# Sorting rounds 1 to 3 of a mixture of experts in two sets of four blocks, beside a recurrent mixer, on one Trainium2 core

## What is computed

```python
xn = layernorm(x)
# mixer
prev = shift_by_one_token(xn); xx = prev - xn
lin = lambda mix, W: (xn + xx * mix) @ W.T          # six of them: r, w, k, v, a, g
r, alpha, g = sigmoid(...), sigmoid(...), sigmoid(...); decay = exp(-softplus(...)); k = tanh(...)
state = state * decay + alpha * k * v               # along the 256 tokens of a sequence
mixed = r * state
mn = group_norm(mixed, 16 groups of 8 channels) * gn_w + gn_b
s = (mn * g) @ W_out.T + b_out
# experts
cur = xn
for r in range(4):
    logits = cur @ Wg[r] + bg[r]
    cw = softmax over the best two logits, 0 for the other two experts
    y_e = gelu(cur @ W1[e] + b1[e]) @ W2[e] + b2[e]  # for each expert e
    cur = cur + sum_e cw[:, e] * y_e
out = x + s * silu(cur)
```

## Time and profile before

| | us |
|---|---|
| runs, median of 3 | 808.48 (805.29 to 808.94) |
| profiled execution | 802.44 |
| its span | 800.7 |
| PE busy in the span | 757.6 |
| DVE, ACT busy | 623.9, 613.9 |
| POOL busy | 198.8 |

### The profile page before, as it was taken

One profiled execution on the slowest core, in us unless ns is written; L12 is line 12 of the kernel. 1 busy time (PEld: TensorE's weight loads), 2 busy tenths in 40 slices (PEclk: granted clock), 3 DMA queues, 4 the chain that ended last, 5 costly groups with the idle time before them and its releaser, 6 DMA issues.

```text
span 800.7 us, 9933 instructions
## 1 busy us (share of the span) xinstructions
PE 757.6 (95%) x3250; PEld 591.2 (74%) x3250; DVE 623.9 (78%) x1035; ACT 613.9 (77%) x858; POOL 198.8 (25%) x223
## 2 busy tenths in 40 slices
PE   8999999999999999999999999999889799758796
PEld 7778777877877777787788778777666677646675
DVE  7999876897896897788788689857699378568456
ACT  7989787887887887788788778778577687466574
POOL 1122111111111111111111111111563016555844
PEclk9999999999999999999999999999979999969898
DMA  8567965332644326533264322644113869949742
GB/s 261 145 120 185 229 154 113 56 97 40 158 107 94 52 40 145 120 92 53 56 143 106 93 39 52 160 100 100 42 41 114 234 197 282 309 130 266 197 128 59
DMA packets 80220, 102.25 MB, mean 128 GB/s; under 512 B 40366, under 2 KB 52138, under 8 KB 76970
## 3 DMA queue, kind: packets, MB, share of 16 engines
q1 hardware_dynamic: 60314, 63.80, 26.3%
q0 software_dynamic: 19440, 37.56, 24.9%
q10 hardware_dynamic: 416, 0.26, 0.1%
HBM read 44.85 MB, written 8.73 MB: 67 GB/s over the span
## 4 chain that ended last, share of the span: by engine, by line
PE 71%; DVE 9%; issue 6%; DMA 4%; ACT 4%; POOL 4%; SPq 1%; POOLq 0%; DVEq 0%; ACTq 0%
PE h_bank L1627 11%; PE h_bank L1631 11%; PE h_bank L1628 11%; PE y_bank L1728 10%; PE y_bank L1716 10%; PE y_bank L1718 10%; PE p_bank L1834 5%; DMA cur<-tmp 4%; DVE g_lo L1294 2%; ACT g L865 2%; ACT g_hi L871 2%; POOL out L744 1%; DVE tmp L1313 1%; POOL cw_b L735 1%; PE r_bank L1766 1%
## 5 line engine op out<-in xcount | busy, mean ns | idle before, releaser
L1294 DVE TENSOR_TENSOR g_lo<-g,g_hi 128x1024 fp32r<-128x1024 f32 x242 | 292.6, 1222 | 142.4 <-ACT g_hi L871 139.6
L865 ACT ACTIVATE g<-h_bank,b_all 128x512 f32<-128x512 f32 x416 | 265.8, 681 | 55.4 <-PE h_bank L1631 54.7
L871 ACT ACTIVATE g_hi<-g 128x1024 fp32r<-128x1024 f32 x242 | 256.8, 1061 | 7.6
L775 POOL DMA_DIRECT2D cur<-tmp x96 | 83.4, 869 | 494.1 <-DVE tmp L1313 330.7
L1627 PE MATMUL h_bank<-cur_hi,w_all 128*128 128x512 f32 x416 | 184.2, 443 | 0.2 <-ACT cur_hi L917 0.2
L1631 PE MATMUL h_bank<-cur_lo,w_all 128*128 128x512 f32 x416 | 163.7, 393 | 0.0
L1628 PE MATMUL h_bank<-cur_hi,w_all 128*128 128x512 f32 x416 | 163.4, 393 | 0.0
L1716 PE MATMUL y_bank<-g_hi,w_all 128*128 128x512 f32 x408 | 157.5, 391 | 0.0
L1718 PE MATMUL y_bank<-g_hi,w_all 128*128 128x512 f32 x392 | 152.6, 389 | 0.0
L1728 PE MATMUL y_bank<-g_lo,w_all 128*128 128x512 f32 x408 | 111.1, 393 | 4.4 <-DVE g_lo L1294 4.4
L1627 PEld LDWEIGHTS h_bank<-cur_hi,w_all 128*128 128x128 f32 x416 | 78.7, 189 | 32.7 <-issue 17.3
(11 more groups left out here) (238 smaller groups left out, 733.8 us busy)
## 6 DMA issues: line engine op xcount, KB each, us to landing
cur<-tmp POOLq DMA_DIRECT2D x113, 256.0 KB
cw_b<-cw_scratch SPq DMA_DIRECT2D x25, 1024.0 KB, 5.8
staged<-w_all SPq DMA_DIRECT2D x34, 512.0 KB
cw_b<-sorted_gates SPq DMA_DIRECT2D x17, 256.0 KB
xn_t<-cur SPq DMA_DIRECT2D x8, 256.0 KB, 5.9
cur<-in_x SPq DMA_DIRECT2D x7, 256.0 KB, 5.3
bench<-sorted_rows SPq DMA_DIRECT2D x6, 266.0 KB, 6.1
xn_scratch<-bench POOLq DMA_DIRECT2D x6, 256.0 KB, 3.1
```

The costliest lines, as they stand in the source:

```text
L775: pool.dma_start(cur[:, block_of(turn_of(s))], tmp[:, s % SUMS, :], accum_op=ALU.add).then_inc(summed, DMA)
L865: nc.scalar.activation(g[:, gb, ft * BLK:(ft + 1) * BLK], hb[ft][:, :], ACT.Gelu_apprx_tanh, bias=bias_of(s1, ft)).then_inc(gelu_done, 1)
L871: nc.scalar.activation(g_hi[:, gb, h], g[:, gb, h], ACT.Copy).then_inc(g_hi_done, 1)
L1294: nc.vector.tensor_tensor(g_lo[:, gb, h], g[:, gb, h], as_f32(g_hi[:, gb, h]), ALU.subtract).then_inc(g_lo_done, 1)
```

## The change

Rounds 1 to 3 are all sorted, in two **sets** of four blocks (blocks 0 to 3 and 4 to 7), so there are six sorts (`SORTS`), n = 0 to 5; sort n is for set n % 2 in round n // 2 + 1. Each list has 2 x 4 + 5 = 13 items (`LIST`) where four blocks have 16 steps. Round 0 stays dense: steps 0 to 31. The six lists follow, steps 32 to 109. While the list of one set runs, the other set is sorted: `after(n)` is the last step whose sum set n needs, and every part of sort n stands at a fixed distance behind it, the first item at `after(n) + 14`. With it come these changes:

- Mixers start every 10 steps; all eight `s` go to memory as rows, and all of the output is written by scatters.
- ACT writes `cur_hi` of a block that comes back, straight from the bank (`take_back`); DVE writes only `cur_lo`. ACT takes the squares of the group norm (`squares`) and its scale and shift (`scale_normed`), with waits of DVE on ACT and of ACT on DVE in between.
- DVE adds no sums any more: POOL does all, and scatters the four tiles of one block in each of four steps.
- Ranks stand at `after + 3` between the two halves of low parts, pairs and scores behind `combine` of that step, gates and places behind `combine` of the next, the list at `after + 6`. The places are scanned over 96 counts and not 144, `match` has 208 elements and not 408.
- PE loads 13 slot numbers ahead of `down` two steps before each list (`load_slots`); SP loads 13 expert and 13 gate numbers, POOL 13 block numbers, for each list.
- Gathers of `s` and `x` for set 0 stand behind steps 87, 88, 91 and 92, those for set 1 behind 100 to 103.

The diff, cut:

```diff
-SORTED = 6
-ITEMS = 2 * SORTED + 5
-TURNS = R * NB - SORTED
-FIRST_ITEM = E * (TURNS - 1)
-LAST_AT = FIRST_ITEM + ITEMS
-STEPS = LAST_AT + E
+SET = 4
+SORTS = 2 * (R - 1)
+LIST = 2 * SET + 5
+ITEMS = SORTS * LIST
+FIRST_ITEM = E * NB
+STEPS = FIRST_ITEM + ITEMS
...
-MIX_AT = (15, 26, 37, 48, 59, 70, 84, 102)
+MIX_AT = tuple(15 + 10 * m for m in range(NB))
...
-BATCHES = [(0, 2), (2, 2)] + [(k, QUADS) for k in range(QUADS, TURNS - 2, QUADS)] + [(TURNS - 2, 1), (TURNS - 1, 1)]
+BATCHES = [(0, 2), (2, 2), (4, QUADS)]
...
+def sums_for(n, j):
+    return E * (SET * n + j + 1) if n < 2 else first_step(n - 2) + items_through(j)
+
+def after(n):
+    return sums_for(n, SET - 1) - 1
...
+SORT_AT = {n: after(n) + 2 for n in range(SORTS)}
+PAIR_AT = {n: after(n) + 3 for n in range(SORTS)}
+PLACE_AT = {n: after(n) + 4 for n in range(SORTS)}
+LIST_AT = {n: after(n) + 6 for n in range(SORTS)}
+ROW_AT = {(n, j): after(n) + 4 + j for n in range(SORTS) for j in range(SET)}
+BACK_END = {(n, j): after(n) + (11, 12, 13)[j // 2 + j % 2] for n in range(SORTS) for j in (0, 1, 3)}
+BACK_MID = {(n, 2): after(n) + 13 for n in range(SORTS)}
+GATES_AT = {(n, h): after(n) + 12 + 2 * h for n in range(SORTS) for h in range(2)}
+SPLIT_SORTED_AT = {(n, j): after(n) + (12, 13, 15, 16)[j] for n in range(SORTS) for j in range(SET)}
+SILU_AT = {(n, j): first_step(n) + items_through(j) + 1 for n in (SORTS - 2, SORTS - 1) for j in range(SET)}
+SILU_AT.update({(SORTS - 2, j): first_step(SORTS - 1) + j - 1 for j in (1, 2, 3)})
+SILU_AT[SORTS - 1, SET - 1] = None
...
+GATHER_AFTER = {(SORTS - 2, 0): 87, (SORTS - 2, 1): 88, (SORTS - 2, 2): 91, (SORTS - 2, 3): 92,
+                (SORTS - 1, 0): 100, (SORTS - 1, 1): 101, (SORTS - 1, 2): 102, (SORTS - 1, 3): 103}
...
             for s in range(STEPS - ADDED_BY_DVE):
...
-                if s in ADDED_BY_DVE_AT:
-                    continue
...
                 pool.wait_ge(combined, s + 3)
                 if s > 0:
+                    pool.wait_ge(summed, DMA * s)
+                for n in range(SORTS):
+                    if s == first_step(n):
+                        pool.wait_ge(listed, n + 1)
+                        regs = [pool.alloc_register(f"block{n}_{i}") for i in range(LIST)]
+                        pool.load(regs, tables[0:1, n % 2, T_BLOCK, 0:LIST])
...
+                for n, j in at_step(ROW_AT, s):
+                    scatter_rows(n, j)
+                for n, j in at_step(SILU_AT, s):
+                    pool.wait_ge(row_out, OUT_ORDER.index((n, j)) + 1)
+                    scatter_out(n, j)
+                for n, j in at_step(GATHER_AFTER, s):
+                    gather_sx(n, j)
...
-            def take_back(j):
+            def take_back(n, j):
...
+                nc.scalar.activation(cur[:, block_of(SET * (n % 2) + j)], rb[:, :], ACT.Copy)
...
+                nc.scalar.activation(cur_hi[:, q, :], rb[:, :], ACT.Copy).then_inc(r_empty, 1)
...
+            def squares(m):
+
+                act.wait_ge(centred, m + 1)
+                nc.scalar.activation(sq[:, :, :], cen[:, :, :], ACT.Square).then_inc(squared, 1)
+
+            def scale_normed(m):
+
+                act.wait_ge(mn_ready, m + 1)
+                act.wait_ge(dve_consts, 1)
+                nc.scalar.activation(gn[:, :, :], mn_t[:, :, :], ACT.Identity, bias=gnb2[:, :], scale=gnw4[:, :]).then_inc(normed, 1)
...
             def mixer_squares(m):
 
-                link(nc.vector.tensor_tensor(sq[:, :, :], cen[:, :, :], cen[:, :, :], ALU.mult))
+                dve.wait_ge(centred, m + 1)
+                dve.wait_ge(squared, m + 1)
...
+            def load_slots(n):
+
+                regs = [pe.alloc_register(f"slot{n}_{i}") for i in range(LIST)]
+                pe.wait_ge(listed, n + 1)
+                pe.load(regs, tables[0:1, n % 2, T_SLOT, 0:LIST])
...
+                pe.wait_ge(r_empty, bank_job("sort_logits", n))
+                pe.wait_ge(summed, DMA * sums_for(n, SET - 1))
+                tokens = cur[:, n % 2 * SET * BLK:(n % 2 + 1) * SET * BLK].rearrange("p (m i r) -> p i m r", i=D // RP, r=RP)
                 for i in range(D // RP):
+                    last = nc.tensor.matmul(rb[RP * i:RP * (i + 1), :], wg_p[:, n // 2 + 1, :], tokens[:, i, :, :], start=True, stop=True)
```

More of the change, by code:

```diff
@@ L94 @@
 COUNTS = len(PAIRS) * COLS
 ROW = D + E + 1
[L96 to L110, removed]
@@ new lines @@
+SILU_AT[SORTS - 1, SET - 1] = None
+IDS_AT = {n: after(n) + 15 for n in (SORTS - 2, SORTS - 1)}
+GATHER_AFTER = {(SORTS - 2, 0): 87, (SORTS - 2, 1): 88, (SORTS - 2, 2): 91, (SORTS - 2, 3): 92,
+                (SORTS - 1, 0): 100, (SORTS - 1, 1): 101, (SORTS - 1, 2): 102, (SORTS - 1, 3): 103}
+OUT_ORDER = sorted((key for key, s in SILU_AT.items() if s is not None), key=SILU_AT.get)
+MID, END = 0, 1
+BANK_TIMES = {("logits", n, 0): (s, MID if n == 0 else END) for n, s in LOGITS_AT.items()}
+BANK_TIMES.update({("sort_logits", n, 0): (s, MID) for n, s in SORT_AT.items()})
@@ new lines @@
+BANK_TIMES.update({("counts", n, 0): (s, MID) for n, s in PLACE_AT.items()})
+BANK_TIMES.update({("row", n, j): (s, END) for (n, j), s in ROW_AT.items()})
+BANK_TIMES.update({("back", n, j): (s, END) for (n, j), s in BACK_END.items()})
+BANK_TIMES.update({("back", n, j): (s, MID) for (n, j), s in BACK_MID.items()})
+BANK_TIMES.update({("gates", n, h): (s, MID) for (n, h), s in GATES_AT.items()})
+BANK_TIMES.update({("end", n, j): (s, END) for (n, j), s in SILU_AT.items() if s is not None})
+assert len(set(BANK_TIMES.values())) == len(BANK_TIMES)
@@ L357, in block_of @@
         def block_of(k):
[L358 to L368 removed]
+            return slice(k * BLK, (k + 1) * BLK)
         def unit_of_w1(i):
@@ L593, in _, with load_list @@
+            def load_list(n, kind, name):
+                regs = [sp.alloc_register(f"{name}{n}_{i}") for i in range(LIST)]
+                sp.wait_ge(listed, n + 1)
+                sp.load(regs, tables[0:1, n % 2, kind, 0:LIST])
+                return [sp.snap(reg, donate=True, min_val=0, max_val=E - 1 if kind == T_EXPERT else ZEROS) for reg in regs]
             copy_block(0)
@@ L676, in _ @@
+            for key in row_stored:
+                sp.wait_ge(row_stored[key], DMA * TPB)
         @block.gpsimd
@@ L771, in _ @@
                 if is_item(s):
-                    pool.dma_start(cur[:, bass.ds(blocks[s - FIRST_ITEM] * BLK, BLK)], tmp[:, s % SUMS, :],
-                                   accum_op=ALU.add).then_inc(summed, DMA)
-                else:
-                    pool.dma_start(cur[:, block_of(turn_of(s))], tmp[:, s % SUMS, :], accum_op=ALU.add).then_inc(summed, DMA)
-                if s == SORT_LOGITS_AT[1]:
-                    for j in range(1, SORTED):
-                        scatter_rows(j)
@@ L779, in _ @@
-                for j in at_step(SILU_AT, s):
-                    scatter_out(j)
-                for j in at_step(GATHER_AFTER, s):
-                    gather_sx(j)
+                    n, a = item_of(s)
+                    half = cur[:, n % 2 * SET * BLK:(n % 2 + 1) * SET * BLK]
+                    pool.dma_start(half[:, bass.ds(blocks[a] * BLK, BLK)], tmp[:, s % SUMS, :], accum_op=ALU.add).then_inc(summed, DMA)
+                else:
+                    pool.dma_start(cur[:, block_of(s // E)], tmp[:, s % SUMS, :], accum_op=ALU.add).then_inc(summed, DMA)
```

931 lines of the change are left out of this document (388 added, 543 removed).

## The result

| | before | changed kernel |
|---|---|---|
| median of the runs | 807.91 us (4 runs, 805.29 to 808.94) | 819.32 us (4 runs, 814.90 to 821.05) |
| ratio, 95% interval | | 1.0138, 1.0087 to 1.0189 |
| profiled execution, its span | 802.44, 800.7 us | 821.05, 819.3 us |
| mean granted clock | 0.976 | 0.951 |
| TensorE busy | 757.6 us | 729.8 us |

The changed kernel is 1.4% slower. The forecast was 779 us with a range of 752 to 812: sign and range are both wrong. TensorE's instructions did become fewer, as the sum said. It stands more often, and it runs longer at half clock.

A forecast was written before the change was run, and what follows sets the result against it. TensorE's work was taken to bound each step until the last round's sort and items. Eight terms summed to -29.5 us on the 800.7 us span, giving 771.2 and a forecast of 779 us, range 752 to 812.

The forecast's parts named there:

- terms 1 to 3: Whole kernel: 11 fewer steps -60.0 us, router batches -6.8, transposes of rows +15.8 and smaller sort work +3.
- term 2: Router on TensorE: four four-block batches go at 2.4 us each, with single and sort batches changed; together -6.8 us.
- Term 4: TensorE's queue: six register loads of 13 numbers at 3.3 us each replace one costing 6.3; +13.5 us.
- Rival A: Register loads and sorts hide, so terms 4 and 5 shrink and term 6 goes: 743 us, with half 761; chance 0.17.
- term 5: VectorE around each sort: some steps run over, low parts' allowed lateness takes most; 2 us a sort, net +2 us.
- Term 6: Each list's last item: sort_logits waits on TensorE's queue for its landed sum, 0.7 us a sort; +4 us.
- Term 7: Gathers, stores, SiLU: sums some 10 us late at step 92, second place step 105; 28 us for 32, -4 us.
- Term 8: Kernel end: last halves go out by two row scatters each instead of one plain store; +3 us.
- B: Rival: the chain of adds on POOL becomes the bound, 818 us at 7.5 us an add; with C in full 0.13.
- C: Rival: each sort costs what today's does, 845 us, a third of it 801; in part 0.10, with B in full 0.13.
- ScalarE's part as cover: Work moved to ScalarE is no term; without it term 5 would grow by upper parts and mixers' squares and scale.
- the prediction's estimate of over 100 us: POOL scatters: by the skill page's port rule, four scatters would hold each of 24 adds back 12 us; weighed against the trace.

The follow-up runs named there:

- cured kernel: Changed kernel with first-block transposes a step earlier, at most three gathers or stores between adds, and first projections a step later: 769.17 and 768.47 us.
- run 5: On the changed kernel, only the first of each sort's four transposes moved one step earlier, ScalarE emptying the bank at once: 795.72 us, ratio 0.9877.
- run 7: On the changed kernel, a mixer's first projection put a step later, ahead of that step's second layer: 807.59 us, ratio 1.0034.
- Run 6: On the changed kernel, at most three gathers or stores between two adds from step 85, first finished blocks turned at 93 and 106: 804.70 us, ratio 0.9978.
- run 9: VectorE takes back upper parts, squares and scaling: 816.05 us on the changed kernel; 771.88 and 773.59 us with the three order edits.

## Why the prediction was wrong

The forecast for the span was -29.5 us, and it rose by 18.6. TensorE's busy time tells where: it fell by 27.8 us, and by 38.5 with the lower clock's part taken out, where terms 1 to 3 said 48. Its idle time ahead of its last matmul grew by 37.3 us (74.3 for 37.0), the lower clock took 10.7 more, and the time behind the last matmul 9.1 more.

*Terms 1 to 3, steps, router, transposes:* right on the steps, with 5.44 us between `combine` outputs, and too favourable on the router. Term 2 took 2.4 us for a batch from two stretches of the earlier trace rows. The matmuls of a batch lie in the shorter of the two, and none in the longer:

```profile
218.40:283.80 65.40, 1.06 (x8) 0.16 (x8) 1.00 0.41 85
283.80:351.60 67.80, 0.00 (x0) 0.00 (x0) 1.00 0.44 94
```

The longer one is longer by 13 matmuls of `up`. At 1.06 us a batch, term 2 is about -1 and not -6.8. In the cured kernel TensorE is busy for 715 us against "some 710"; in the changed kernel for 729.8, since matmuls at half clock last longer.

*Term 4, register loads, +13.5:* too dear. No stand behind a load is in the list of waits of the changed kernel, so there the term was nearer to -6. In the cured kernel such stands do show, 4.7 and 3.0 us in its two runs, and six extra loads cost 6.6 us. Rival A was right on this term. The error was to scale the one long load by its count of numbers, where SyncE's short one stood beside it in the earlier trace rows.

*Term 5, VectorE around a sort, +2: this is the step that failed.* It asked how long VectorE's pieces last and how late a low part may be for them. It did not ask who else holds the bank. The pieces are as short as it said, and low parts are hardly late. But five small operations stand between `combine` and the release of `r_bank`, with `turn_row` of the same step waiting on TensorE's queue. That is 18.5 us of standing and 11.3 lost at half clock behind it, of which run 5 gave back 21. The same question was not put to `p_bank` when the mixers moved to 10 steps: 7.1 us of standing, 8 in all (run 7), for which the sum has no term.

*Term 6:* 4 us forecast, 4.0 shown.

*Term 7, the end of each set, -4:* the mechanism and its two places (step 92, then 105) were right, and the lateness nearly so: the add of step 90 came 13.5 us late where it said some 10. The size was not. 28.9 us of standing, and half clock that lasts 4.8 us beyond the first long wait, are more than the 28 that it took for both together. And the 32 for the kernel before was too much: in its last 11 steps TensorE worked for 11.6 of 20.5 us at half clock, so 5.8 were lost and not 10. Run 6 gives 13 us for pacing the queue.

*Term 8, the end, +3:* too small. TensorE's last matmul ends 15.2 us before the span does (804.1 of 819.3), against 6.1 us before. GpSimd issues row stores back to back there:

```profile
801.38 1.12 POOL L681 DMA_INDIRECT out<-cw_b,id_i  x1 [0.96 <-DVE cw_b L1218]
...
805.38 0.98 POOL L681 DMA_INDIRECT out<-cw_b,id_i  x1 [0.30 <-DVE cw_b L1228]
...
810.51 0.98 POOL L681 DMA_INDIRECT out<-cw_b,id_i  x1 [0.30 <-issue]
```

The last four, from 806.66 on, are the halves'. They stand behind four of the block before, which waited for VectorE until 801.38. This +9 is in all runs here (9 to 14 us); none tried to shorten it.

*Half clock* was counted only behind register loads and at the end. It came behind each of the six waits on the counts' reader too. In all it costs 22 us, half of the 44.7 in which TensorE works at it, for 12 before.

*The rivals.* B's sign, `sort_logits` waiting for `cur<-tmp` in each list, came in three of six and for 4.0 us; steps without a sort still take 5.44 us. C's price came in part (its third was 801), and one of its two signs: half clock behind each sort, 3.4 us behind five of the six waits and 6.8 behind one. The other did not come: TensorE waited 0.8 us for low parts. What the prediction lacked was a rival of another kind: a wait built into the order by a shared bank. *ScalarE's part as cover* was overstated: taking it away costs nothing in the changed kernel and about 5 us in the cured one (run 9).

With the three waits mended, the kernel takes 768 to 769 us, 10 less than forecast. So most of the loss is one of places in the order. That it ends so near the forecast is in part luck: term 4 was some 15 us too dear there, while terms 2 and 8 were some 6 and 8 too cheap. Left open: what part of the adds' lateness is the transfers' load (DMA share near 1) and what GpSimd's queue; pacing removed over half of the wait.

## What to carry to other kernels

When a change adds users to a shared bank or moves jobs into the same step, write down for each job in the bank's order who empties it, behind which instruction that engine does so, and whether that instruction waits for the one who wants the bank. Such a wait comes even where the engine waited for has time, as VectorE had here, and costs its length and some more through the clock. A queue that issues both dependent adds and bulk indirect transfers needs its issues counted per step against the step's length, and over all the steps in a row, not only in the fullest one.

## What the runs showed of the hardware

- A register load of 13 numbers took 1.34 to 3.30 us in the changed kernel and 1.34 to 4.59 in the cured one, always at the same place of a step, so its count does not set its time alone. A second one behind each cost 1.1 us.
- Of two loads in a row into the same registers, one is missing from the trace: six, not twelve. What leaves it out is not shown.
- Half clock followed a gap of 2.20 us here (724.8 to 727.0), while one of 2.3 before the change was not followed by it (725.10 to 728.50 above), so the length of one gap did not decide it. The Trainium skill (TensorE: Matmul & The Clock Gate, "What's actually happening") ties the clock to how busy the array has been lately, and this trace agrees.
- 96 scatters took 1.04 us as a median and 3.29 at the most, with VectorE busy 72% of the time. The Trainium skill (SBUF — State Buffer, "SBUF: two separate sides") gives about 3.1 us for a GpSimd DMA that meets a copy of VectorE's on their shared port. Only the longest comes near it. The page's case is not this kernel's, where 266.8 of VectorE's 589.9 us are `TENSOR_TENSOR` and not copies, so the prediction's estimate of over 100 us did not hold here, and the page's own case stays untried.

```profile
L652 POOL DMA_INDIRECT sorted_rows<-bench,place_i x96: 977/1036/3289, 146.0 to 675.5; - x96
```
